# A two-layer decoder on one core: x loaded and stored in four transfers inside the first and last stages, head 0's weights split beside the tokens, output bias added behind head 0

## What is computed

```python
xn = (x - mean(x)) / sqrt(var(x) + 1e-5)
for h in range(16):
    q, k, v = xn @ W_Q[h] + b_Q[h], xn @ W_K[h] + b_K[h], xn @ W_V[h] + b_V[h]
    p = softmax(causal(q @ k.T / sqrt(128)))
    x = x + (p @ v) @ W_O[h]
x = x + b_O
```

## Time and profile before

| | |
|---|---|
| three runs | 1788.96, 1783.52, 1783.42 us; median 1783.52 |
| the profiled execution | 1782.1 us |
| its span, first to last instruction | 1780.3 us |
| TensorE matmul busy | 1593.2 us (89% of the span) |
| VectorE, ScalarE, GpSimd busy | 1089.6 us (61%), 864.7 us (49%), 671.8 us (38%) |
| mean granted TensorE clock | 0.962 of full speed |
| moved by DMA | 70.26 MB, 39 GB/s on average |

### The profile page before, as it was taken

How to read it: one execution, slowest core, us unless ns; L and a number is a source line. 1 busy time by engine, 2 the same in 40 slices (tenths; PEclk the granted TensorE clock), 3 DMA queues, 4 the chain that set the end, 5 groups by cost and what they waited for, 6 DMA issues and landing times. The chain is left out here.

```text
span 1780.3 us, 37048 instructions
## 1 busy us (share of the span) xinstructions
PE 1593.2 (89%) x14668; PEld 1284.0 (72%) x14668; DVE 1089.6 (61%) x1746; ACT 864.7 (49%) x1466; POOL 671.8 (38%) x527
## 2 busy tenths in 40 slices
PE   4999999999996887799999787999986898999997
PEld 3888888888885565677788464566663675888886
DVE  6667767677776888566442558999993564111111
ACT  2555545555452665555422346667662663322222
POOL 0021121211212562531422155999992430323232
PEclk9999999999997998899999789999997997999999
DMA  3011111111112200000101120000002800000001
GB/s 103 16 54 60 42 62 50 41 62 59 43 51 93 91 2 26 8 12 10 40 25 80 43 48 1 2 2 1 2 2 107 287 2 1 1 1 1 1 0 47
DMA packets 71391, 70.26 MB, mean 39 GB/s; under 512 B 24624, under 2 KB 64176, under 8 KB 70624
## 3 DMA queue, kind: packets, MB, share of 16 engines
q1 hardware_dynamic: 71264, 68.46, 12.0%
HBM read 46.03 MB, written 19.27 MB: 37 GB/s over the span
## 5 line engine op out<-in xcount | busy, mean ns | idle before, releaser
L624 POOL TENSOR_TENSOR s_w_parts<-s_w_raw,s_w_parts 128x768 fp32r<-128x768 f32 x16 | 29.7, 1856 | 429.4 <-ACT s_w_parts L576 429.4
L1426 DVE TENSOR_TENSOR s6f_hid<-s6f_act_sb,s6f_u_ps 128x512 f32<-128x512 f32 x64 | 44.0, 688 | 219.4 <-PE s6f_u_ps L1377 219.4
L1449 POOL TENSOR_TENSOR s6f_hid_parts<-s6f_hid,s6f_hid_parts 128x512 fp32r<-128x512 f32 x64 | 82.6, 1291 | 226.0 <-ACT s6f_hid_parts L1415 226.0
L2157 POOL TENSOR_TENSOR s4b_with_q<-s4b_with_q 128x1024 f32<-128x1024 f32 x64 | 150.8, 2379 | 0.6 <-DVE s4b_with_q L2120 0.6
L2120 DVE TENSOR_TENSOR s4b_with_q<-s4b_c_ps,s_q_rows 128x2048 f32<-128x2048 f32 x64 | 146.1, 2284 | 0.8 <-PE s4b_c_ps L2251 0.7
L500 PE MATMUL s_v_ps<-s_wv_parts,s_xnT 128*128 128x256 f32 x768 | 104.7, 286 | 12.1 <-ACT s_v L605 6.5
L559 PE MATMUL s_o_ps<-s_w_parts,s_zT 128*128 128x256 f32 x768 | 110.0, 293 | 3.7 <-DVE x_rows L663 3.7
L1415 ACT ACTIVATE s6f_hid_parts<-s6f_hid 128x512 fp32r<-128x512 f32 x64 | 40.5, 632 | 145.0 <-PE s6f_o_ps L1397 140.8
L500 PEld LDWEIGHTS s_v_ps<-s_wv_parts,s_xnT 128*128 128x128 f32 x768 | 97.1, 191 | 17.7 <-ACT s_v L605 9.7
L1397 PEld LDWEIGHTS s6f_o_ps<-s6w_parts,s6f_hid_parts 128*128 128x128 f32 x768 | 99.2, 188 | 6.8 <-issue 1.0
L559 PEld LDWEIGHTS s_o_ps<-s_w_parts,s_zT 128*128 128x128 f32 x768 | 96.8, 192 | 8.5 <-issue 4.3
(11 more groups left out here) (324 smaller groups left out, 3992.8 us busy)
## 6 DMA issues: line engine op xcount, KB each, us to landing
stored_weights<-s1q_halves SPq DMA_DIRECT2D x16, 768.0 KB, 3.7
s6w_parts<-stored_weights SPq DMA_DIRECT2D x32, 384.0 KB, 8.0
s1q_packed<-in_codes SPq DMA_DIRECT2D x8, 384.0 KB, 4.3
s1q_scale<-in_scale_rows SPq DMA_DIRECT2D x8, 384.0 KB, 4.9
s3p_raw<-in_ffn_pieces SPq DMA_DIRECT2D x8, 384.0 KB, 8.6
early_values<-s_vbd SPq DMA_DIRECT2D x1, 2176.0 KB, 11.4
s_vbd<-early_values SPq DMA_DIRECT2D x1, 2176.0 KB, 12.7
x_rows<-in_x SPq DMA_DIRECT2D x1, 2048.0 KB, 8.4
```

The costliest lines, as they stand in the source:

```text
L1426: nc.vector.tensor_tensor(hid[:, f % 2, :], act_sb[:, f % 2, :], u_ps[:, f % 2, :], ALU.mult) \
L1449: nc.gpsimd.tensor_tensor(hid_parts[:, f % 2, 1, :], hid[:, f % 2, :], hid_parts[:, f % 2, 0, :], ALU.subtract).then_inc(low_done, 1)
L2157: nc.gpsimd.tensor_tensor(with_q[:, half, :, 0, :, n_, :], with_q[:, half, :, 0, :, n_, :], with_q[:, half, :, 1, :, 1 - n_, :], op).then_ ...
```

## The change

The stages `load` and `store` go. x comes in four transfers of four tiles (`X_CHUNK`), issued in `first_loads` ahead of everything else, each with a semaphore of its own; VectorE waits for one ahead of every fourth bn_stats, ScalarE waits for the constants ahead of the square root. The last `feed_forward` gets a part for SP: behind each group's last addition it stores the group's four tiles, and it waits for all four stores. Head 0's weights (and the value weights of heads 0 and 1) are split through the hooks of `split_tokens`; `split_high` and `split_low` skip head 0. bo is loaded behind head 0's weights, and added on VectorE behind `add_out` of units 0 to 3, four tiles at a time; units 4 to 7 wait for that. The other lines of the diff hand names through.

```diff
...
@@ -193,7 +193,10 @@
-def token_stats(core, mv, rstd, tag, rms_eps=None, factor=None, prefetch=None, beside=None):
+X_CHUNK = 4
+
+
+def token_stats(core, mv, rstd, tag, rms_eps=None, factor=None, prefetch=None, beside=None, x_in=None, const_in=None):
     nc = core.nc
     with ExitStack() as ctx:
         room = Room(nc, ctx, tag)
@@ -222,6 +225,8 @@
         def _(dve):
             if not ready:
                 for t in range(NT):
+                    if x_in and t % X_CHUNK == 0:
+                        dve.wait_ge(x_in[t // X_CHUNK], 16)
                     nc.vector.bn_stats(stats[:, t, :], core.x[:, t, :]).then_inc(stats_done, 1)
                 dve.wait_ge(stats_done, NT)
             for t in range(NT):
@@ -244,6 +249,8 @@
         @block.scalar
         def _(act):
             act.wait_ge(mv_done, NT)
+            if const_in:
+                act.wait_ge(const_in, 16)
             nc.scalar.activation(std[:, :], mv[:, :, 1], ACT.Sqrt, bias=core.c("eps_ln")).then_inc(std_done, 1)
             if rms_eps is not None:
                 act.wait_ge(square_done, 2)
@@ -408,9 +415,11 @@
         wv_parts = oroom.sb("wv_parts", [P, 2, NC, 2, E], F32R)
         bias = oroom.sb("bias", [P, 2, 3])
         bo = oroom.sb("bo", [P, D])
-        (w_in0, w_in1, bias_in0, bias_in1, bo_in, o_full, w_low, wv_in, wv_low) = oroom.sems(
-            "w_in0", "w_in1", "bias_in0", "bias_in1", "bo_in", "o_full", "w_low", "wv_in", "wv_low")
+        (bo_added, w_in0, w_in1, bias_in0, bias_in1, bo_in, o_full, w_low, wv_in, wv_low) = oroom.sems(
+            "bo_added", "w_in0", "w_in1", "bias_in0", "bias_in1", "bo_in", "o_full", "w_low", "wv_in", "wv_low")
         w_in, bias_in = (w_in0, w_in1), (bias_in0, bias_in1)
+        x_in = oroom.sems(*[f"x_in{n}" for n in range(NT // X_CHUNK)])
+        (const_in,) = oroom.sems("const_in")
         deq = Dequantiser(core, Room(nc, octx, "s1q"))
         def load(sp, h, rnd, slot):
@@ -433,14 +442,35 @@
                         .then_inc(wv_in, 16)
         def first_loads(sp):
+            rows = ins["x"].rearrange("(t p) d -> p t d", p=P)
+            for n, arrived in enumerate(x_in):
+                tiles = slice(n * X_CHUNK, (n + 1) * X_CHUNK)
+                sp.dma_start(core.x[:, tiles, :], rows[:, tiles, :]).then_inc(arrived, 16)
+            sp.dma_start(core.const[:, :], ins["const"]).then_inc(const_in, 16)
+            load(sp, 0, 0, 0)
             sp.dma_start(bo[:, :], ins["L0_attn_b_O"].rearrange("(a n) -> a n", a=1).to_broadcast([P, D])) \
                 .then_inc(bo_in, 16)
-            load(sp, 0, 0, 0)
             load(sp, 1, 0, 1)
             deq.load(sp, 0)
-        token_stats(core, mv, rstd, "s1n", prefetch=first_loads)
-        split_tokens(core, xnT, mv, rstd, "s1t")
+        token_stats(core, mv, rstd, "s1n", prefetch=first_loads, x_in=x_in, const_in=const_in)
+        w_high, wv_high = oroom.sems("w_high", "wv_high")
+
+        def high_weights(act):
+            act.wait_ge(w_in[0], 48)
+            nc.scalar.activation(w_parts[:, 0, 0, :, :], w_raw[:, 0, :, :], ACT.Copy).then_inc(w_high, 1)
+            act.wait_ge(wv_in, 32)
+            nc.scalar.activation(wv_parts[:, 0, :, :, :], wv_raw[:, :, :, :], ACT.Copy).then_inc(wv_high, 1)
+
+        def low_weights(pool):
+            pool.wait_ge(w_high, 1)
+            nc.gpsimd.tensor_tensor(w_parts[:, 0, 1, :, :], w_raw[:, 0, :, :], w_parts[:, 0, 0, :, :],
+                                    ALU.subtract).then_inc(w_low, 1)
+            pool.wait_ge(wv_high, 1)
+            nc.gpsimd.tensor_tensor(wv_parts[:, 1, :, :, :], wv_raw[:, :, :, :], wv_parts[:, 0, :, :, :],
+                                    ALU.subtract).then_inc(wv_low, 1)
+
+        split_tokens(core, xnT, mv, rstd, "s1t", beside=low_weights, high_beside=high_weights)
         with ExitStack() as ctx:
             room = Room(nc, ctx, "s1")
             qT = room.sb("qT", [P, TG * P])
...
@@ -568,7 +597,7 @@
                 def split_high(u, rnd, k):
-                    if k % G != 1:
+                    if k % G != 1 or (isinstance(u, int) and u == 1):
                         return
                     slot = k // G
                     act.wait_ge(w_in[slot], (rnd + 1) * 48)
@@ -620,6 +649,8 @@
             @block.gpsimd
             def _(pool):
                 def split_low(h, rnd, slot):
+                    if isinstance(h, int) and h == 0:
+                        return
                     pool.wait_ge(w_high, h + 1)
                     nc.gpsimd.tensor_tensor(w_parts[:, slot, 1, :, :], w_raw[:, slot, :, :], w_parts[:, slot, 0, :, :],
                                             ALU.subtract).then_inc(w_low, 1)
@@ -635,11 +666,6 @@
             def _(dve):
                 nc.vector.memset(prob[:, :, :], 0.0).then_inc(zeroed, 1)
                 dve.wait_ge(zeroed, 1)
-                dve.wait_ge(bo_in, 16)
-                for t in range(NT):
-                    last = nc.vector.tensor_tensor(core.x[:, t, :], core.x[:, t, :], bo[:, :], ALU.add)
-                last.then_inc(zeroed, 1)
-                dve.wait_ge(zeroed, 2)
                 def z_low_part(u, rnd, k):
                     dve.wait_ge(z_high, u + 1)
@@ -659,10 +685,18 @@
                 def add_out(u, rnd, k):
                     dve.wait_ge(o_full, u + 1)
+                    if isinstance(u, int) and G <= u < 2 * G:
+                        dve.wait_ge(bo_added, u - G + 1)
                     t0 = (k % G) * TG
                     nc.vector.tensor_tensor(core.x[:, t0:t0 + TG, :], core.x[:, t0:t0 + TG, :],
                                             o_ps[:, :, :].rearrange("p b (t n) -> p (b t) n", t=2), ALU.add) \
                         .then_inc(o_out, 1)
+                    if isinstance(u, int) and u < G:
+                        dve.wait_ge(bo_in, 16)
+                        dve.wait_ge(o_out, u + 1)
+                        nc.vector.tensor_tensor(core.x[:, t0:t0 + TG, :], core.x[:, t0:t0 + TG, :],
+                                                bo[:, :].unsqueeze(1).to_broadcast([P, TG, D]), ALU.add) \
+                            .then_inc(bo_added, 1)
                     if isinstance(u, int) and u >= U - G:
                         dve.wait_ge(o_out, u + 1)
                         for t in range(t0, t0 + TG):
...
@@ -1344,6 +1378,18 @@
             @block.sync
             def _(sp):
                 early.sync(sp)
+
+        if out is not None:
+            stored = room.sems("stored")[0]
+
+            @block.sync
+            def _(sp):
+                rows = out.rearrange("(t p) d -> p t d", p=P)
+                for g in range(G):
+                    tiles = slice(g * TG, (g + 1) * TG)
+                    sp.wait_ge(o_out, g + 1)
+                    sp.dma_start(rows[:, tiles, :], core.x[:, tiles, :]).then_inc(stored, 16)
+                sp.wait_ge(stored, 16 * G)
         def split_modulation(engine_is_scalar, eng):
@@ -2487,7 +2533,7 @@
         zT = room.sb("zT", [P, 2, NC, NT, P], F32R)
         token_stats(core, mv, rstd, "s6n")
         split_tokens(core, zT, mv, rstd, "s6t", column_step=2)
-        feed_forward(core, "s6f", zT, w.gate, w.up, w.down, F, ACT.Gelu_apprx_tanh, ready=w.ready)
+        feed_forward(core, "s6f", zT, w.gate, w.up, w.down, F, ACT.Gelu_apprx_tanh, ready=w.ready, out=core.out)
@@ -2548,35 +2594,10 @@
 def decoder(nc, ins, out):
     with ExitStack() as ctx:
-        core = Core(nc, ctx, ins)
-        run_stage(core, load)
+        core = Core(nc, ctx, ins, out)
         for n, stage in STAGE.items():
             if n in STAGES:
                 run_stage(core, stage)
-        run_stage(core, lambda core: store(core, out))
-
-
-def load(core):
-    with ExitStack() as ctx:
-        (x_in,) = Room(core.nc, ctx, "ld").sems("x_in")
-        block = ctx.enter_context(core.nc.Block())
-
-        @block.sync
-        def _(sp):
-            sp.dma_start(core.x[:, :, :], core.ins["x"].rearrange("(t p) d -> p t d", p=P)).then_inc(x_in, 16)
-            sp.dma_start(core.const[:, :], core.ins["const"]).then_inc(x_in, 16)
-            sp.wait_ge(x_in, 32)
-
-
-def store(core, out):
-    with ExitStack() as ctx:
-        (stored,) = Room(core.nc, ctx, "st").sems("stored")
-        block = ctx.enter_context(core.nc.Block())
-
-        @block.sync
-        def _(sp):
-            sp.dma_start(out.rearrange("(t p) d -> p t d", p=P), core.x[:, :, :]).then_inc(stored, 16)
-            sp.wait_ge(stored, 16)
 STAGE = {"1": stage_L0_attention, "2": stage_L0_cross_and_ffn, "4": stage_L1_attention,
```

More of the change, by code:

```diff
@@ L133, with __init__ @@
 class Core:
-    def __init__(self, nc, ctx, ins):
-        self.nc, self.ins, self.ctx = nc, ins, ctx
+    def __init__(self, nc, ctx, ins, out):
+        self.nc, self.ins, self.ctx, self.out = nc, ins, ctx, out
         self.cols, width = constant_columns()
@@ L464, in stage_L0_attention @@
             (q_full, k_full, v_full, s_full, pT_full, z_full, q_out, k_out, v_out,
```

(7 more changed lines are left out.)

## The result

Four runs of each kernel: before 1785.18 us (1783.42 to 1788.96), after 1770.21 us (1769.42 to 1770.71), a ratio of 0.9916 with the interval 0.9898 to 0.9935. In six more runs beside eleven of the kernel before it was 0.9927 (0.9903 to 0.9950). The change makes the kernel about 0.8% faster, some 13 to 15 us; the two intervals together reach from 9 to 18 us. The profiled execution took 1769.42 us with a span of 1767.6; the forecast was 1769.9 and 1768.1.

The account below looks back on a forecast made before the run. TensorE paces the heads, so microseconds taken from the first 35 us should move everything behind. Terms -5.8 - 4.2 + 2.5 + 0.5 - 5.2 = -12.2 us took 1783.5 to 1771.3 us, range 1767.0 to 1776.5.

Parts of the forecast that it names:

- x, load stage: Kernel start: x in four transfers, no load stage, brings the first normalisation to 12.8 us; -5.8 us.
- detour: Token split in stage 1: lengthened by splitting head 0's weights beside it; +2.5 us (0.8 to 3.1).
- gap to the head: Between last token split and TensorE's first head matmul: 4.62 us shrinks to 0.4; -4.2 us.
- bias: Head 0, units 0 to 3: additions on VectorE make TensorE slip; +0.5 us (0 to 1.2).
- tail: Kernel end: store in four, only the last 512 KB exposed behind the last addition; -5.2 us (-4.5 to -5.4).
- rival (b): Start: the four x transfers don't flow into each other, x there at 12.4 us; +3.2, 1774.5 us; chance 0.03.
- SP: Barrier ending the statistics: SP's last issue ends about 10, maybe 12 us, holding nothing; 0, kept 0 to +1 us.
- rival (a): Statistics barrier: SP, pushed back by its queue, holds it, tokens start 4.4 us later; 1775.7 us; chance 0.07.
- Stage 4 as a model: Stage 4's token split with the same detour, 3.1 us longer than stage 1's, scaled to +2.5 us.
- second slow group: TensorE's first head matmuls: possibly a second slow group, 1.35 us more; taken as 0.
- (c): Pairs of heads: lasting VectorE lag makes operations collide with GpSimd; 26 us, 1797 us; chance 0.03.
- (d): First heads: waits half lose the head's gain, all upper bounds; 1779 us; chance 0.05.

Follow-up runs that it names:

- act_order: Changed kernel with the dequantiser's two ScalarE copies issued ahead of the exponent instead of behind it; 1772.1 us, ratio 0.9933 to the kernel before.
- again_after: The changed kernel run and traced a second time, no edit; 1768.2 us, ratio 0.9927 to the kernel before.
- again_before: The kernel before, run again for a second trace, no edit; 1787.0 us in one run.
- one_x: Changed kernel with x in one 2 MB transfer inside the stage instead of four; 1774.2 us in one run.
- no_split: Changed kernel with head 0's weight split and the bias as before, x and store as changed; 1774.9 us in one run.
- split_only: Kernel before with only head 0's weights split beside the tokens; 1779.0 us in one run.
- store_only: Kernel before with only the four stores in the last stage and no store stage; 1777.4 us, ratio 0.9972.
- best: Changed kernel with the bias ahead of the first unit and ScalarE's weight copies ahead of the first token tile; 1766.7 us, ratio 0.9918 to before.

## Why the prediction was right, step by step

| term | forecast | measured | from |
|---|---|---|---|
| x, load stage | -5.8 | -5.4 | first normalisation 13.19 |
| detour | +2.5 | +1.9 | token split 13.76 us for 11.83 |
| gap to the head | -4.2 | -4.1 | 0.48 us for 4.62 |
| bias | +0.5 | +1.45 | lead, 69 to 100 us |
| tail | -5.2 | -5.1 | 3.8 us for 8.9 |
| sum | -12.2 | -11.3 | |
| span | -12.2 | -12.7 | |

**x.** Right, with one detail off: the last piece came 0.4 us later than one transfer (9.6 for 9.16). VectorE starts on the first at 5.01 and on the third at 8.06, where 4.5 and 7.5 were forecast. The page of the Trainium skill that was weighed, DMA: Bandwidth & Descriptors (Rules for kernel authors), asks for 1 MiB per transfer; its price here was these 0.4 us (0.1 to 0.9 over the traces) against 3.4 gained, so rival (b) fell, which had x there at 12.4. Every piece had further transfers queued behind it; what pieces cost a load with nothing behind them was not measured. The constants were nearer to costing something than forecast: they landed at about 10.9 us instead of 10.35, and the function table that ScalarE loads behind them was in place at 12.24, 0.1 us behind the statistics (12.16) that the square root waits for.

**SP.** Its last issue ended at 11.65 us, inside the estimated 10 to 12, and VectorE waited 0.34 us at the barrier, as before: rival (a) fell. The push-back was there (the constants 0.70, the two value weights 1.46 us), just not enough.

**The detour.** Stage 4 as a model was 1.2 us too dear (3.1 for 1.9; scaled by GpSimd's times alone it gives 2.7, not the 2.5 taken): the two stretched normalisations, 0.87 and 1.02 us, lost 1.1 together, ScalarE's copies 0.8 (VectorE's wait at 21.54). One normalisation of 2.35 us, as there, didn't occur, and the trace shows what sets the size. Each stretched one ends 0.15 us behind the subtraction of GpSimd beside it: 22.75 behind 22.60 (20.79 + 1.81), 24.02 behind 23.88, and in stage 4 of before 1010.71 behind 1010.56. There it had begun 0.14 us behind the start of a subtraction of 2.34 us; here 0.7 and 0.9 us of the subtractions were left. **The gap** went as forecast. The slow first matmuls stayed as they were, 2.90 us; the second group's up to 1 us more, with no wait, lies within the 1.35 us that the prediction left for a second slow group.

**The bias** is the step that failed. VectorE's lag was sized well: the additions of units 1 to 4 (63.66, 71.03, 78.46, 85.82 against 70.79, 77.55, 84.33, 91.16, with 7.6 taken off) lag by 0.5, 1.1, 1.7 and 2.3 us, where 0.7, 1.35, 2.0 and 2.65 stood in the text. The direct wait for unit 3's addition was right too: 0.4 us, once act_order bared it. Two claims were wrong. That TensorE is reached only through its own waits for VectorE: ScalarE's order reached it first, though act_order shows that the total does not hang on this one wait. And that VectorE's idle 3.65 us ahead of L2401 would take the lag up: that pause ends when GpSimd is done, and GpSimd had become late by the same lag; it shrank to 2.84 us, so 0.8 us went and 1.4 stayed. The measured loss lies above the bound of 1.2 that the text set. Rivals (c) and (d) fell: from 150 to 546 us the lead stays within 0.2 us in after and grows by 1.0 in again_after, so no pair of heads got longer, and 5.2 to 5.8 us of the head's 7.0 to 7.6 are left at 150 us.

**The sum** is 0.9 us poorer than forecast, and 0.3 us more were gone at 150 us, as in again_before. That the span still came out 0.5 us better than forecast is the middle of that one trace, where the lead grew by 1.8 us (5.8 at 150 us, 7.6 at 1700) without an edit; again_before lost 4.6 us there. In whole runs the head (5.2 to 5.8 us at 150 us) and the tail (5.1) make 10.3 to 10.9 us, inside the second comparison's interval and 0.7 us short of the first's; the rest of the 13 to 15 us was traced to nothing that was edited, and may be noise. Each part of the sum is shown by runs of its own (x by one_x and no_split, detour and gap together by split_only, the bias by four runs, the tail by store_only); the closeness of the total is partly chance.

## What to carry to other kernels

Ahead of a pipeline's start each microsecond counts in full; the time there could be summed from waits, each term within 0.1 to 0.6 us. Inside a pipeline, work added to an engine with idle time reaches the bounding engine by the orders of the other engines, not only by its direct waits: follow what stands behind each late instruction on each queue, and check whether a pause that is to absorb the lag is itself ended by something late. Measure changes of 1 to 3 us in the stretch where they act; whole runs of the same code spread by up to 10 us here.

## What the runs showed of the hardware

Four queued 512 KB transfers brought 2 MB in 0.1 to 0.9 us more than one, over nine traces, and gave the first tiles about 4.2 us earlier (5.01 for 9.16). Two normalisations beside GpSimd's subtractions took 0.87 to 0.90 and 1.02 us instead of 0.40 in every run that has both, early among the tokens (best) or late, and ended 0.15 us behind the subtraction beside them. TensorE's first twelve matmuls behind the token split took 2.90 us in every trace, the six behind them 1.63 to 2.76 us with a granted clock shown as 1.00, for 1.54 later on. And the granted clock of one stretch of stage 4 was 0.85, 0.90 or 0.95 with nearly the same instructions, beside a difference of up to 2 us.
